# A 64-item decoder kernel without set-up blocks: constants, cleared keys and early weights made inside the pipeline of the first items

## The reference, cut to what matters

```python
def _layernorm(x): return (x - mean(x)) / sqrt(var(x) + 1e-5)

def reference(x, ctx, mask, ...):                       # x: 16 x 256 x 128, ctx: 16 x 64 x 96
    # self attention, 16 heads of 8: relu(x @ W + b) for Q, K, V; keys whose token sums to 0
    # and keys after the query are hidden; softmax; rows of such tokens zeroed; plus x; normalised
    x = _layernorm(x + self_attention(x))
    # attention against 64 context rows; queries under the mask attend evenly
    x = _layernorm(x + cross_attention(x, ctx, mask))
    y = x
    for l in range(2):
        y = y + causal_attention(_ln(y), ...)           # with an output projection
        h = _ln(y)
        moe = token_moe if l % 2 == 0 else seq_moe      # top 2 of 8 experts, 128 -> 512 -> 128
        y = y + moe(h, ...)
    return _layernorm(x + y)
```

## Time and profile before

| | us |
|---|---|
| median of 3 runs | 1434.69 (1431.61 to 1435.11) |
| the profiled execution's own time | 1435.11 |
| its span in the profile | 1433.1 |
| PE busy | 1224.0 (85%) |
| DVE busy | 934.4 (65%) |
| ACT busy | 778.1 (54%) |
| POOL busy | 685.6 (48%) |

### The profile page before, as it was taken

One profiled execution on the slowest core, in us unless ns is written; L12 is line 12 of the kernel. 1 busy time (PEld: TensorE's weight loads), 2 busy tenths in 40 slices (PEclk: granted clock), 3 DMA queues, 4 the chain that ended last, 5 costly groups with the idle time before them and its releaser, 6 DMA issues. The chain is left out here.

```text
span 1433.1 us, 30001 instructions
## 1 busy us (share of the span) xinstructions
PE 1224.0 (85%) x9702; PEld 984.6 (69%) x9702; DVE 934.4 (65%) x2791; ACT 778.1 (54%) x1591; POOL 685.6 (48%) x1215
## 2 busy tenths in 40 slices
PE   0699999998888689999997399992799999988997
PEld 0477777766666467777775289882576777767886
DVE  6579999877666878888883211112788888744553
ACT  0166676764555356666663155551366666664443
POOL 2255655564222147777777100003577667444554
PEclk9999999986878789999996599996599999999999
DMA  2677775423555544555431377763555555434764
GB/s 51 184 227 232 216 225 158 130 80 109 159 145 136 141 115 124 139 134 138 129 82 31 96 210 220 216 192 88 152 149 144 150 145 135 121 116 142 202 200 120
DMA packets 206510, 210.77 MB, mean 147 GB/s; under 512 B 44819, under 2 KB 158995, under 8 KB 206356
## 3 DMA queue, kind: packets, MB, share of 16 engines
q1 hardware_dynamic: 189476, 187.49, 48.2%
q10 hardware_dynamic: 12784, 12.98, 3.1%
q0 software_dynamic: 4096, 8.40, 2.1%
HBM read 121.84 MB, written 84.41 MB: 144 GB/s over the span
## 5 line engine op out<-in xcount | busy, mean ns | idle before, releaser
L1212 POOL TENSOR_SCALAR_AFFINE_SELECT probs<-probs 128x256 f32<-128x256 f32 (+1 forms) x576 | 280.6, 493 | 242.8 <-ACT probs L902 238.6
L902 ACT ACTIVATE probs<-weights 128x512 f32<-128x512 f32 x448 | 264.7, 598 | 115.2 <-PE weights L714 82.0
L1058 DVE TENSOR_REDUCE negmax<-scores 128x4 f32<-128x512 f32 x384 | 260.7, 685 | 70.4 <-PE scores L662 58.0
L662 PE MATMUL scores<-keys,queries 128*128 128x512 f32 (+1 forms) x384 | 188.7, 498 | 7.6 <-DMA queries<-zeros 3.8
L902 ACT ACTIVATE probs<-weights,keybias 128x512 f32<-128x512 f32 x192 | 131.8, 688 | 70.7 <-PE weights L714 51.5
L714 PE MATMUL weights<-queries,keys 104*128 104x256 f32 x768 | 160.0, 292 | 0.6 <-issue 0.6
L714 PEld LDWEIGHTS weights<-queries,keys 104*128 104x128 f32 x768 | 141.5, 196 | 21.2 <-issue 3.2
L1294 POOL DMA_INDIRECT out_room<-expert_rows,y_index x64 | 63.6, 994 | 192.8 <-POOLq L1548 180.3
L1062 DVE TENSOR_REDUCE negmax<-scores 128x2 f32<-128x512 f32 (+1 forms) x192 | 130.8, 685 | 35.1 <-PE scores L668 24.8
L719 PEld LDWEIGHTS weights<-queries,keys 104*128 104x128 f32 x768 | 115.1, 196 | 14.6 <-ACT probs L902 4.6
L719 PE MATMUL weights<-queries,keys 104*128 104x128 f32 x768 | 110.5, 268 | 3.8 <-ACT probs L902 3.8
(11 more groups left out here) (256 smaller groups left out, 2767.0 us busy)
## 6 DMA issues: line engine op xcount, KB each, us to landing
windows<-parts SPq DMA_DIRECT2D x192, 192.0 KB
queries<-windows SPq DMA_DIRECT2D x64, 384.0 KB
keys<-windows SPq DMA_DIRECT2D x192, 96.0 KB
hidden_room<-in_m_w SPq DMA_DIRECT2D x71, 256.0 KB, 2.7
out_room<-in_m_w SPq DMA_DIRECT2D x71, 256.0 KB, 3.2
routed_rows<-zeros SPq DMA_DIRECT2D x64, 256.0 KB, 3.5
windows<-parts ACTq DMA_DIRECT2D x64, 120.0 KB
xin<-routed_rows SPq DMA_DIRECT2D x39, 128.0 KB, 2.9
```

Source lines behind the costliest of these rows:

```text
L662: i = pe.matmul(bank[:], queries[0:rows, s, t * P:(t + 1) * P], keys[0:rows, s::S4, half * P:(half + 1) * P], start=True, stop=True)
L902: act.activation(probs[:, n % RING], weight_banks[n % 2][:], ACT.Exp, scale=SCALE, **bias).then_inc(exp_done.sem, 1)
L1058: i = dve.tensor_reduce(most[:, part, s, :], bank[:].rearrange("p (a k) -> p a k", k=P), AX.X, ALU.max, negate=True)
L1212: pool.affine_select(out=block, in_=block, compare_op=ALU.is_ge, fill=0.0, base=0, pattern=[[0, heads], [1, P]], channel_multiplier=-1).th ...
```

## The change

It removes both set-up blocks, with the barriers at their ends. What they did is put into the streams of the first attention block as further generators, with slots of their own:

- SP fetches the first tokens as its first instruction; then comes the DMA that places the low bias rows, then the fetch of item 1.
- ACT issues the bias rows and the six loads that the first stage needs (`act_first`: three weights, one bias, `a_gamma`, `a_beta`), and later the 30 other loads (`act_late`), three to a slot. The late loads leave SP's stream. PE waits for the first loads and the low rows before item 0's projection, and for the others before item 16's.
- DVE splits the bias rows first. The clearing of each key buffer and the ones in it are a generator `dve_keys(dve, n)`, begun at slots -20, -11 and -7. SP waits for `keys_made` before it stacks item 0, 1 and 2.
- POOL makes all constants in `pool_setup`, in four portions, straight in their float32r form (no copies by DVE), the columns of ones in `V` and `VX` too, with a wait between dependent writes. `pads` is converted by POOL at item 16.
- `sp_clear`, `pool_hiding` and ACT's write of item 1's values wait for `rest_made`, the scores of item 0 and the ones in the keys for `ready_made`.
- `HIDE` is -2^100 where it was -1.0e30.

```diff
-                for dst, src in early:
-                    sp.dma_start(dst, src).then_inc(sem_setup_dma, 16)
...
-                for n in range(LANES):
-                    dve.memset(K[n][:].bitcast(F32), 0.0)
...
-                dve.wait_ge(sem_setup_dma, 16 * len(early))
-                dve.tensor_copy(pads[:], pad8[:])
...
+            if g < LANES:
+                sp.wait_ge(keys_made, g + 1)
...
+            if g == 0:
+                pe.wait_ge(sem_first_dma, 16 * len(first))
+                pe.wait_ge(low_rows_placed, 16)
+            if g == B:
+                pe.wait_ge(sem_late_dma, 16 * len(late))
...
+        def act_first(act):
+            act.dma_start(loaded_rows, ins["rows"][:, 0:rows]).then_inc(bias_rows_loaded, 16)
+            for dst, src in first:
+                act.dma_start(dst, src).then_inc(sem_first_dma, 16)
+            yield
+
+        def act_late(act):
+            for n, (dst, src) in enumerate(late):
+                act.dma_start(dst, src).then_inc(sem_late_dma, 16)
+                if n % 3 == 2:
+                    yield
...
+        def dve_keys(dve, n):
+
+            step(dve.memset(K[n][:].bitcast(F32), 0.0))
+            cleared = dve_steps[0]
+            yield from rest(2)
+            dve.wait_ge(dve_step, cleared)
+            dve.wait_ge(ready_made, 1)
+            ones_against_maxima(dve, n).then_inc(keys_made, 1)
+            yield
...
+            def values(n):
+                done(pool.memset(VX[n][:], 0.0))
+                done(pool.memset(V[n][:], 0.0))
+                wait()
+                for b in range(2):
+                    done(pool.memset(V[n][:, :, 8 * b:8 * b + 8, 16 * b + DH:16 * b + DH + 1], 1.0))
+                    wait()
+                    done(pool.memset(VX[n][b * TC:(b + 1) * TC, :, 16 * b + DH:16 * b + DH + 1], 1.0))
+                    wait()
...
+            pool.memset(ones_row[:], 1.0).then_inc(ready_made, 1)
+            yield from rest(8)
+            values(1)
+            yield
+            values(2)
+            yield
...
+            return [(-30, 0, act_first(act)), (-13, 2, act_late(act))]
...
+            return [(-25, 0, dve_bias_rows(dve)), (-20, 2, dve_keys(dve, 0)), (-11, 3, dve_keys(dve, 1)), (-7, 3, dve_keys(dve, 2))]
...
+            return [(-30, 0, pool_setup(pool)), (0, 3, pool_hiding(pool))]
```

More of the change, by code:

```diff
@@ L45 @@
 BIG = float(2 ** 32)
-HIDE = -1.0e30
+HIDE = -(2.0 ** 100)
 LANES = 3
@@ L294, in ones_against_maxima @@
             return i
[L296 to L302, removed]
-                for dst, src in early:
-                    sp.dma_start(dst, src).then_inc(sem_setup_dma, 16)
[L306 to L319, removed]
-                for n in range(LANES):
[L321 to L351, removed]
-                    dve.memset(K[n][:].bitcast(F32), 0.0)
[L353 to L375, removed]
-                dve.wait_ge(sem_setup_dma, 16 * len(early))
-                dve.tensor_copy(pads[:], pad8[:])
-                dve.tensor_copy(row_parts[0:1, :], loaded_rows).then_inc(sem_setup, 1)
-                dve.wait_ge(sem_setup, 2)
-                dve.tensor_tensor(low_rows, loaded_rows, row_parts[0:1, :].bitcast(F32),
-                                  ALU.subtract).then_inc(sem_setup, 1)
-                dve.wait_ge(sem_setup, 3)
@@ L1217, in pool_prepare @@
             x, seq = xin[g % LANES], g % B
+            if g == B:
+                pool.wait_ge(sem_late_dma, 16 * len(late))
+                pool.tensor_copy(pads[:], pad8[:]).then_inc(setup_step, 1)
+                pool.wait_ge(setup_step, setup_steps[0] + 1)
             pool.wait_ge(fetched.sem(g), fetched.at(g))
@@ L1310, in place @@
                                         pattern=[[1, P]], channel_multiplier=-HIDE_KEYS))
-            done(pool.memset(hidden_room[:, 0:2 * P], 0.0))
-            yield
+            pool.wait_ge(rest_made, 1)
             for n in range(HIDE_KEYS):
@@ L1336, in pool_stages @@
                     (U.outputs + 9, 1, pool_last))
-        def attention(items, extra=(), pool_extra=(), behind=None):
-            of = behind or [lambda eng: []] * 6
-            def emit(eng, stages, more=()):
-                interleave([(first_slot[g] + at, rank, stage(eng, g)) for g in items for at, rank, stage in stages(g)] + list(more))
+        setup_steps = [0]
+        def act_first(act):
[3 more added lines that the diff above has]
+            yield
@@ L1345, in attention, with emit @@
+        def attention(items, others, last):
+            def emit(eng, stages, more):
+                interleave([(first_slot[g] + at, rank, stage(eng, g)) for g in items for at, rank, stage in stages(g)] + more)
             with nc.Block() as block:
```

113 lines of the change are left out of this document (91 added, 22 removed).

## The result

The changed kernel took 1421.61 us (median of 4, 1419.54 to 1422.69), the kernel before 1433.15 (4 runs, 1431.48 to 1435.11) on the same chip: ratio 0.9907, 95% interval 0.9882 to 0.9931. The forecast was 1421.0 in 1414 to 1428, "faster" at 0.92. The profiled execution took 1422.69 us, span 1421.0. The number is right; two of the things behind it are not, and they offset each other. Compared with the prediction's sum, the start gained more than forecast, and a stage in the middle lost some of it again, which it did not do in every execution.

The account below looks back on a forecast made before the run. PE sets the pace once the pipeline is full, so only the start counts: item 1's scores 14.2 us earlier, less 0.2 for PE's clock, make 14.0 off 1435.1, so 1421.1 (1420.7 on the median), range 1414 to 1428.

Parts of the forecast that it names:

- Start: Up to item 0's `tok`: tokens landed at 2.9 us, bias rows done at 4.4, `tok` at 6.2.
- Keys of item 0: Clearing and ones on DVE: POOL ready at 10.8 us (10.4 to 11.5), item 0's split at 13.6.
- POOL ahead of item 1's masks: POOL's constants between item 0's high parts and item 1's masks: 7.6 us, masks at 23.0, item 1's `tok` at 23.5.
- DVE ahead of item 1's split: Ones, a clearing and ones on DVE after `tok`: 9.8 us, item 1's split at 33.3 instead of 45.02.
- Item 1's scores: From windows' store to item 1's scores: 12.8 us, scores at 47.9 instead of 62.12, 14.2 earlier.
- PE's clock at the start: Low-clock stretch behind PE's idle time between items 0 and 1: 0.2 us off the gain, bounds 0 and 2.5.
- signs that the prediction named for being wrong: ACT issues far beyond 0.47 us holding `keeprows` beyond 30; item 1's scores outside 46 to 52; a later stage several microseconds longer.
- the loads collide: Rival, 13%: ACT's loads share DMA engines with item 0's transfers, its scores at 32.7 us, absorbed; with backlog, gain 11 us, 1424.1.
- POOL and the waits are dearer: Rival, 18%: every bound at the start at its dear end, gain 8.7 us, 1426.4.
- The whole preamble: Rival, 4%: the 27.3 us before item 0 vanish with nothing in their place, 1407.8 us.
- The clock: Rival, 3%: PE at 1.2 GHz for 40 us of work after the altered filling, a loss of 26 us, 1461.
- no later stage: Rival, 5%: a later stage not moving with PE gives the gain back, or it is not done; 1431 to 1439 us.

Follow-up runs that it names:

- run 3: Changed kernel with the third key buffer cleared twice on DVE, ahead of item 1's split: 1417.71 us, ratio 0.9915.
- runs 4 and 7: Changed kernel edited: 4, POOL makes item 1's masks before its other constants, 1416.08 us; 7, third key buffer cleared on DVE behind item 1's split, 1421.20 us.
- run 5: Changed kernel with the 30 late loads moved from ACT's queue to SP's, one to a slot: 1428.59 us, ratio 0.9982.
- run 6: Kernel before with only the first two token fetches moved to the head of SP's queue, both set-up blocks kept: 1436.04 us, ratio 0.9995.
- runs 8 and 9: 8 has its own line under run 8; 9 is 8 with `ctxT` and `pad` behind SP's second fetch, other 27 loads from slot 130: 1407.98 us, ratio 0.9836.
- run 8: Changed kernel with ACT clearing second and third key buffers, item 1's masks first on POOL, the 30 late loads on SP from slot 40: 1416.01 us, ratio 0.9889.

## Why the prediction was right, and where it was not

*Start.* Right: bias rows done at 4.2 (4.4), `tok` at 5.9 (6.2).

*Keys of item 0.* The order was right, one term too dear. POOL was ready at 9.71, against 10.8 and a cheap bound of 10.4; 0.3 of that came from masks that were done earlier. The term that failed is the wait between dependent instructions, 0.09 to 0.24: with tiny writes of 0.11 to 0.13 it is about 0.05. A chain of selects was not the like of a chain of writes. The split came at 12.99 (13.6), limited by DVE itself, which the prediction had only as the fast side of its range.

*POOL ahead of item 1's masks.* 6.75 us (14.76 to 21.51) against 7.6 and a cheap bound of 7.1 (its own terms add up to 7.2 to 8.7, not 7.1 to 8.9), by the same error: 1.98 per item (14.70 to 16.68) where I had 2.1 to 2.9. It brought `tok` to 22.0 (23.5).

*DVE ahead of item 1's split.* Right: 10.0 from `tok` to the split (9.8), and run 3 shows the queue to be the cause in full. On ACT "nine issues of 0.47" failed: the issue behind `pad` took 3.38. ACT stood 0.8 us short of deciding, and runs 4 and 7 show it as the next bound.

*Item 1's scores.* 11.37 from the store (12.8 taken). In three executions of the one kernel it was 11.4 to 12.7, so the term holds at its low end. Together: scores at 45.25 to 46.55 (47.9), of the 2.7 us in the first execution 1.3 by the split and 1.4 by this term.

*PE's clock at the start.* The sum took off 0.2 for it; instead the lead grew by 0.3 to 1.1 between item 1's scores and item 10 (16.9 to 17.5, 16.2 to 17.3, 15.6 to 15.9). Small, as forecast, but of the other sign.

*The sum.* The start gave 17.5, 17.3 and 15.9 us in three executions (0.8 more if the second execution of the kernel before is the measure); forecast were 14.0. What brought the profiled execution to 12.4 us of gain all the same was the stage of items 10 to 32, at the clock of 0.78. The three medians of this one kernel lie 11.5, 18.8 and 15.7 below the kernel before beside them, 15.3 on average. The forecast of 14.0 holds for the change to 1.3 us; that it met the first median to 0.6 was luck. The range stood for one measurement; the second one, 1412.39, lies outside it. The stage's own scatter was no term of the range and should have been, with some 4 us either way (270.1 to 278.0 in one kernel). Of the signs that the prediction named for being wrong, two came: item 1's scores stood ahead of 46 in two of three executions, and a later stage was longer by several microseconds. A third came half: an issue lasted far beyond 0.47, but `keeprows` was done by 26.

*The rivals.* That the loads collide happened as that rival said: item 0's scores at 31.32 (32.7 by it), 26.03 without the loads (run 5), and the maxima still wait for item 1's split, so it was absorbed. The rule of the Trainium skill named there ("DMA: Bandwidth & Descriptors", section "Issuing engines are not separate DMA queues") agrees: with the loads on ACT's queue item 0's relay on SP's took 16.48 us, without them 11.19 (14.84 to 26.03, run 5). "POOL and the waits are dearer" was wrong in sign: they were cheaper. The whole preamble did not go: run 3 prices what remained. The clock did not take the gain back, and no later stage did, though one took 4.9 us of it in the profiled execution.

## What to carry to other kernels

A set-up ahead of the first item counts against the whole time when one engine sets the pace from there on: what the start gained was still there at item 10. Here taking the set-up apart paid, and moving the first fetch alone gave nothing (run 6). What is left is set by the queue ahead of the second item's critical step, so give the long clearings to the engine that idles there, and put loads with many small pieces where their queue has nothing else to issue (runs 8 and 9; on SP among the items' transfers the same loads took back 10 of the 17 us at item 10, run 5). Before explaining a few microseconds in a stage that the change doesn't touch, run the same kernel again and compare the granted clock of that stage.

## What the runs showed of the hardware

- How long an issue lasts depends on what stands ahead of it. `m_gw` took 2.63 to 3.46 us on ACT's queue directly behind `pad` in seven executions, and 2.48 on SP's (run 5), where 0.45 to 0.84 is usual. `pad` itself took 2.67 to 3.66 behind `ctxT`, but 0.43 in run 5 and 1.76 in run 8. ACT did nothing else meanwhile; what in the queue holds the issue is not shown.
- PE's granted clock over the same 1670 matmuls was 0.78, 0.83 and 0.78 in three executions of one kernel, and the stretch lasted 278.0, 270.1 and 277.4 us; over the two executions of the kernel before it was 0.79 and 0.81, with 273.1 and 271.6. PE alternates there between its two levels (the stretch from 430 to 460 above was at the lower, 0.50, throughout); what tips it was not found.
- A write of 128x16 on POOL took 0.13 us and the next, behind a wait, started 0.18 after its start. ACT fills 128x4096 in 3.56 us by a copy, DVE in 3.47 with 0.80 to 0.92 of idle time before it.
